# A fused vision-and-text block on one core: the products of the identity that fill TensorE's waits are left out

## What is computed

```python
h = tok(x, W, b, cls_token, pos_embedding)             # patches @ W.T + b, class token, positions
h = concatenate([h, txt], axis=1)                      # 32 x 69 x 256
h = h + attn0(layernorm(h))                            # rotary softmax attention, 16 heads of 16
h = h + ffn0(layernorm(h))                             # 8 experts of 128, top 2 by sigmoid gate, and a shared one
h = h + attn1(layernorm(h))                            # linear attention, layernorm, feed 256-1024-256, layernorm
h = h + ffn1(layernorm(h))                             # 8 experts of 1024, top 2 by softmax
```

## Time and profile before

| | |
|---|---|
| median of three runs | 1016.52 us (1016.45 to 1018.35) |
| the profiled execution | 1020.34 us, of which its span 1018.1 us |
| granted TensorE clock, mean | 0.971 |
| PE busy | 926.0 us, 91% of the span |
| ACT, DVE, POOL busy | 58%, 57%, 62% |

### The profile page before, as it was taken

One profiled execution on the slowest core, in us unless ns is written; L12 is line 12 of the kernel. 1 busy time (PEld: TensorE's weight loads), 2 busy tenths in 40 slices (PEclk: granted clock), 3 DMA queues, 4 the chain that ended last, 5 costly groups with the idle time before them and its releaser, 6 DMA issues. The chain is left out here.

```text
span 1018.1 us, 21166 instructions
## 1 busy us (share of the span) xinstructions
PE 926.0 (91%) x6820; PEld 845.2 (83%) x6820; DVE 576.7 (57%) x1326; ACT 588.6 (58%) x1243; POOL 632.5 (62%) x632
## 2 busy tenths in 40 slices
PE   6997999997999999789879999978999999999980
PEld 5884777776899988579869999867999999999980
DVE  1548999976766663498633666555333333333334
ACT  0432777775666664487445666523766666666644
POOL 3575888875555544253259987611777777778760
PEclk9999999998999999899999999979999999999995
DMA  8773444431311120000080000083566666666657
GB/s 320 250 249 84 148 160 154 159 115 38 110 64 55 47 80 9 1 1 2 1 337 2 17 16 17 16 342 122 158 201 190 198 187 203 206 195 194 192 177 272
DMA packets 66775, 134.60 MB, mean 132 GB/s; under 512 B 12809, under 2 KB 29364, under 8 KB 65524
## 3 DMA queue, kind: packets, MB, share of 16 engines
q1 hardware_dynamic: 58126, 116.49, 35.3%
q0 software_dynamic: 4032, 11.02, 3.0%
q10 hardware_dynamic: 4550, 6.24, 1.8%
HBM read 111.56 MB, written 23.21 MB: 132 GB/s over the span
## 5 line engine op out<-in xcount | busy, mean ns | idle before, releaser
L122 DVE CAST place<-place 128x512 fp32r<-128x512 f32 (+1 forms) x168 | 88.3, 567 | 155.7 <-PE moe_down L128 80.3
L2529 POOL TENSOR_TENSOR place<-place,place 128x512 fp32r<-128x512 f32 x84 | 138.0, 1643 | 50.4 <-DVE place L122 44.7
L2555 PE MATMUL moe_up<-place,place 128*128 128x128 f32 x1344 | 157.0, 275 | 0.5 <-ACT place L2654 0.5
L2555 PEld LDWEIGHTS moe_up<-place,place 128*128 128x128 f32 x1344 | 153.4, 192 | 0.8 <-ACT place L2654 0.8
L128 PE MATMUL moe_down<-place,place 128*128 128x256 f32 x1008 | 132.6, 288 | 4.6 <-DMA place<-w_remainder 2.7
L128 PEld LDWEIGHTS moe_down<-place,place 128*128 128x128 f32 x1008 | 124.8, 193 | 5.1 <-issue 5.1
L2671 ACT ACTIVATE place<-moe_up,place 128x128 f32<-128x128 f32 x336 | 95.1, 367 | 19.0 <-POOL place L2529 14.7
L2658 ACT ACTIVATE place<-place 128x2048 f32 x42 | 80.3, 1913 | 22.4 <-issue 13.1
L1500 POOL TENSOR_TENSOR place<-place,place 128x384 fp32r<-128x384 f32 x42 | 43.9, 1048 | 64.9 <-ACT place L1372 45.0
L1052 PE MATMUL ff_down<-place,place 128*128 128x256 f32 x486 | 69.6, 289 | 4.6 <-POOL place L1500 3.9
L1052 PEld LDWEIGHTS ff_down<-place,place 128*128 128x128 f32 x486 | 61.7, 189 | 11.5 <-POOL place L1500 9.6
(11 more groups left out here) (320 smaller groups left out, 2040.8 us busy)
## 6 DMA issues: line engine op xcount, KB each, us to landing
place<-w_remainder SPq DMA_DIRECT2D x168, 256.0 KB
place<-in_w_dram SPq DMA_DIRECT2D x4, 4096.0 KB, 13.4
place<-gate_rows SPq DMA_DIRECT2D x24, 384.0 KB, 4.9
place<-in_w_dram SPq DMA_DIRECT2D x16, 512.0 KB, 3.7
w_remainder<-place SPq DMA_DIRECT2D x16, 512.0 KB, 2.9
place<-choices SPq DMA_DIRECT2D x5, 768.0 KB, 7.5
place<-value_rows SPq DMA_DIRECT2D x56, 64.0 KB, 2.3
place<-in_patches_dram SPq DMA_DIRECT2D x8, 384.0 KB, 5.6
```

The lines of the kernel that those rows point to most:

```text
L122: return eng.tensor_copy(out, x)
L2529: pool.tensor_tensor(lo[f], raw[f], hi[f].bitcast(F32), ALU.subtract).then_inc(h_split, 1)
L2555: last = pe.matmul(p1[u][k // HK][:, (k % HK) * P:(k % HK + 1) * P], ws[u][:, c, k * P:(k + 1) * P], xT[u][:, c, :], start=(c == 0), stop= ...
```

## The change

All calls of `keep_busy` go, and with them the function. That makes 96 products: 4 at A, 3 at B, 5 at C, 10 at D, 6 at E, 12 at F, 24 at G, 22 at H and 10 at I. Waits, DMAs and the other engines' code stay as they are.

```diff
-def keep_busy(pe, bank, ident, rows, count, fresh=True):
-    for _ in range(count):
-        pe.matmul(bank[:, 0:D], ident, rows, start=fresh, stop=fresh, skip_group_check=True)
...
                         proj(n + 2 - NB)
                         if n == NB - 1:
                             pe.wait_ge(summed, 1)
-                        busy(up[:, 0 if n == NB - 2 else 2, :], 2)
...
                 flip_x(0)
                 pe.wait_ge(summed, 2)
-                busy(up[:, 0, :], 3)
                 logits(0)
                 for n in range(R):
                     rise(n)
                 fall(0)
                 turn_gates(0)
-                busy(turn[:, 1, :], 2)
                 flip_x(1)
-                keep_busy(pe, po[:, 1, D:2 * D], self.ident, self.wo0[:, 0, :], 3, False)
                 logits(1)
...
-                keep_busy(pe, up[:, 0, :], self.ident, self.wo0[:, 0, :], 10)
                 flip_out(NG - 1)
...
                 pe.wait_ge(preset, 7)
-                keep_busy(pe, pc, self.ident, self.wo1[:, 0, :], 6)
                 for a in range(NT + 8):
...
                 proj(0)
                 proj(1)
-                busy(po[:, 0, :], 10)
                 flip_x(0)
-                busy(po[:, 0, :], 2)
                 for n in range(R):
                     rise(n)
...
                 for g in (NG - 2, NG - 1):
-                    busy(up[:, 0, :], 6 if g == NG - 2 else 16)
                     flip_out(g)
-                    busy(up[:, 0, :], 1)
                     logits(g)
...
                 for k in range(2):
-                    keep_busy(pe, idle, self.ident, self.h[:, 0, :], 20 if k == 0 else 2)
                     pe.wait_ge(hot_ready, k + 1)
...
-                keep_busy(pe, p2, self.ident, self.h[:, 0, :], 10)
                 turn_x(0, 0, 0)
                 rise(0, 0)
```

More of the change, by code:

```diff
@@ L1063, in bias_down @@
                         pe.matmul(thirds(po, j), gt_parts[0:3 * ROWS, j * P:(j + 1) * P], e2_b_parts[0:3 * ROWS, :], start=False, stop=False, skip_group_check=True)
-                def busy(bank, count):
-                    keep_busy(pe, bank, self.ident, self.wo0[:, 0, :], count)
                 scores(0)
@@ L2009, in fall @@
                     last.then_inc(fall_mm, 1)
-                def busy(bank, count):
-                    keep_busy(pe, bank, self.ident, self.wo1[:, 0, :], count)
                 proj(0)
                 proj(1)
-                busy(po[:, 0, :], 10)
                 flip_x(0)
-                busy(po[:, 0, :], 2)
                 for n in range(R):
```

## The result

The changed kernel takes 1022.52 us (median of six, 1020.9 to 1023.87), against 1017.09 us for the kernel before (median of six, 1016.45 to 1019.33, the three shown above among them). The ratio is 1.0037, 95% interval 1.0021 to 1.0054: 3.8 us slower, 2.1 to 5.5. The direction is as forecast and the forecast difference, +3.5, lies within the interval. The time itself, 1022.52 us, is 2.5 us above the forecast of 1020.0 and only just inside the range that ended at 1022.6.

A forecast was written before the change was run, and what follows sets the result against it. TensorE, busy nine tenths of the 1018.1 us span, was taken to bound the kernel. The terms A to I summed to +3.5 us, which on the median of 1016.52 gave 1020.0 us, range 1016.6 to 1022.6.

The forecast's parts named there:

- A: Last two sequences of attention, two products after each output projection: both pairs lie on the path, -1.7 us.
- B: Three products before logits(0): covered, and a 4.33 us wait for the gates covers even a slow ramp, 0.
- C: Two products after turn_gates(0), three before logits(1): bias products, rise(4) and proj(2) run at half clock, +1.7 us (0 to 2.7).
- D: Ten products before the last flip_out: nothing won, the turn runs at half clock, +0.6 us (0 to 0.9).
- E: Six products ahead of project(0) in linear attention: on the path behind a 5.20 us wait, -3.1 us.
- F: Second feed, ten products before flip_x(0), two behind: slow turn and rises, partly taken up by waits, +1.2 us (0.6 to 2.2).
- G: 24 products at the second feed's end: last two groups' turns and logits slow, all in one chain, +2.9 us (1.3 to 3.4).
- H: 22 products in the routing: both waits are VectorE's, second half of the table may double, +0.3 us (0 to 0.6).
- I: Ten products starting the routed experts: they hold PE up 0.5 us, but rise(0) stands in the ramp, +1.6 us (0.3 to 2.7).
- rival (1): Only long still waits, not thin stretches, bring the clock down: sum +0.2, 1016.7 us, no change; chance 0.25.
- Rival (2): PE's low clock hardly reaches the path: with no price at all the sum is -4.8, 1011.7 us; chance 0.08.
- Rival (3): Ramps at C, F and I take 2.7 us each, A wins only 0.9: +6.1, 1022.6 us; chance 0.17.

The follow-up runs named there:

- the first experiment: Only the products at A and E left out, the other 86 kept, against the kernel before: 1015.33 against 1020.27 us, ratio 0.9955.
- covered products left out: Products at B, C, D, F, G, H and I left out, A and E kept, against the kernel before: 1027.77 against 1020.27 us, ratio 1.0068.
- the combined version: Against the kernel before: A left out, eight products ahead of the wait at E, eight instead of ten at I; 1010.95 against 1018.24 us, ratio 0.9932.
- the thin kernel: At G, 39 products of 8 columns replace the 24 of 256 columns, against the kernel before: 1027.66 against 1018.24 us, ratio 1.0087.

## Why the prediction was right, and where its terms were off

What each place cost, by the shift of the instruction behind it in the changed kernel, beside the single-place runs:

| place | forecast | changed kernel | by itself |
|---|---|---|---|
| A | -1.7 | -1.7 | -1.7 |
| B | 0 | +0.4 | |
| C | +1.7 | +1.9 | +1.4 |
| D | +0.6 | +0.7 | |
| E | -3.1 | -3.2 | -3.9 |
| F | +1.2 | +0.7 | +0.7 |
| G | +2.9 | +2.6 | +2.6 |
| H | +0.3 | +0.4 | |
| I | +1.6 | +2.0 | +2.7 |
| sum | +3.5 | +3.8 | |

The last column has A and E from the one run that leaves both out; B, D and H were not left out by themselves. C is read at 270.29, where its +2.3 and +1.7 at 263.22 have settled. That the column of the changed kernel adds up to the same 3.8 as the timed ratio is partly luck, since the ratio's interval is 3.4 us wide. And that it comes within 0.3 of the forecast sum is partly luck as well: F and G were too dear by 0.8 together, B, C, D, H and I too cheap by 1.2. The mechanism at each place, though, is what was forecast: products on the path cost their length, and the low clock costs where real work stands in the ramp and no wait takes it up.

**A and E** held: idle products directly behind a wait on the path cost their own length, and at half clock twice that. That the products were what cost at these places is shown in both directions, by leaving them out (-4.6) and by doubling them (+4.1 in the trace). The forecast of E also had its mechanism right that the projections slow down when the products go; with the clock kept by products ahead of the wait the place is worth -5.2 us in the trace, 1.3 to 2.0 us more than leaving them out (-3.9 in the first experiment, -3.2 in the changed kernel).

**C, D and H** came out as worked out in the trace of the changed kernel; only C was also timed alone, and cost more (+3.0) than its trace shows, which is open. **B** was taken as covered, and the wait of 4.4 us did cover PE's slow rises; the +0.4 is in VectorE's chain that makes the gates and may have nothing to do with the clock.

**F** was mis-sized at its last step, "a few short waits behind it take a little more: +1.2". Two traces show +0.7. The rises took 1.8 to 2.0 us longer, and the waits for GpSimd at fall(0) and fall(1) took all of it: the waits behind the first were worth 0.8, not 0.3.

**G** held in its sum. Of its four pieces the turn of group 4 kept full clock here and with G alone left out (+0.3 was half a chance; with all covered products left out it ran slow, +0.5), and the logits took 2.73 us at half clock where 2.8 had been worked out from a mixed row.

**I** was too low: the ramp there measured 2.4 us (6.28 against 3.84) and 2.8 us alone, where 2.1 was taken as the middle of 1.5 to 2.7. The ramp stands wholly in rise(0). The other part of the term, 0.5 us by which the ten products held PE up, isn't shown. The prediction took the bias load as what the first turn's copy needs besides; the turn itself waits for the gathered rows. With the products gone it began 4.62, 4.94 and 5.64 us after GpSimd began the gather, in the changed kernel, with I alone left out and with the covered products left out, and 6.59 us after it in the combined version; in the kernel before it was 5.35. So the rows came later or sooner by 2 us with the gather's code unchanged, and that stands in each reading at I.

Two slips of the prediction move nothing: twelve times 0.43 is 5.2, not 5.1, and rival (1) is given as 1016.7 in one place and 1016.6 in the other.

**What else differs between the two traces is not from the change.** The two profiled executions differ already at the embedding, where no product was removed: in these windows, the first of the kernel before and the second of the changed one, PE retires 18 and 9 products of the same kind in the same time.

```profile
12.79:16.19 3.40, 3.40 (x18) 2.99 (x17) 0.42 (x1) 0.29 (x2) 2.29 (x4) 1.00 0.90 334
```

```profile
12.79:16.19 3.40, 3.40 (x9) 2.68 (x9) 0.42 (x1) 0.56 (x2) 2.36 (x4) 1.00 0.84 316
```

The changed kernel's profiled execution left the half rate later and was 1.9 us late from there on. (The column PEclk prints 1.00 for both; it shows no low clock ahead of the first change that the trace records, and the count of products shows the rate.) In linear attention it won 1.6 us, since the half clock of before at 498.43 was absent, and in the routed experts another 1.0. A further 0.9 was won just ahead of G, by a chance of order between VectorE and GpSimd, in rows of the kernel before and then of the changed one:

```profile
654.57 1.02 POOL L2223 TENSOR_TENSOR place<-place,place 128x384 fp32r<-128x384 f32 x1 [1.39 <-ACT place L2158]
654.59 1.82 DVE L2103 TENSOR_TENSOR place<-place,place 128x768 f32<-128x768 f32 x1
```

```profile
653.88 1.84 POOL L2202 TENSOR_TENSOR place<-place,place 128x384 fp32r<-128x384 f32 x1 [1.39 <-ACT place L2137]
653.88 0.96 DVE L2082 TENSOR_TENSOR place<-place,place 128x768 f32<-128x768 f32 x1
```

The two instructions start within 0.02 us of each other. In each trace one of them takes about 1 us (0.96 or 1.02) and the other 1.82 or 1.84. The long one is VectorE's in the kernel before, and the next normalisation follows from it; in the changed kernel it is GpSimd's. The profiled executions of the kernel with I alone left out and of the combined version gained the same 0.9 us there. All this adds up to -1.2 us with smaller steps, which takes the +3.8 of the places to the 2.6 us between the spans; it is no merit of the forecast.

**The rivals.** Rival (1), that thin stretches leave the clock up, had 0.25 and is refuted: by the thin products at G (0.50 for 17.40 us with PE busy for 16.82), and C alone speaks against it as well: once its five products were gone the clock, fallen ahead of the turn of gates, didn't return until 259.64, and from that turn (248.44) on no wait of PE was longer than 1.60 us. The Trainium skill's rule ("TensorE: Matmul & The Clock Gate", section "Why this matters for your kernels"), that idle gaps beyond some 3 us between bursts halve the clock, fits the long waits at D and F: in the changed kernel it fell at 408.73 within a wait of 5.62 us and at 521.37 within one of 5.82. The wait of 6.96 us at I says nothing of it, since the clock had been low there since 661.31. By that rule the thin kernel, with no wait at G over 1.94 us, would have kept its clock there, and the trace doesn't agree. Rival (2), a clock without a price, is refuted by the covered products alone: +6.9 where it gave -0.5. Rival (3), dearer ramps, was true at I (2.4 to 2.8 us) and false at F (1.8 to 2.0, all taken up by waits) and at A (-1.7).

## What to carry to other kernels

Idle products keep the clock without a price only where they stand ahead of the wait and end before it; behind a wait that sets the path they cost their own length, twice that when the clock is already low. Cost each place by two questions, what real work stands in the ramp behind it and which wait behind that takes the loss up, rather than by the number of products. Products of 8 columns filled the time here but did not hold the clock, and in the one trace at hand filling a wait closer went with a longer wait behind it, so the last place of a chain has to be checked as well.

## What the hardware showed that was not expected

The clock stayed at half while PE issued mostly 8-column products (16.82 of 17.40 us busy). The fall and the return of the clock land at different places from one execution to the next of nearly the same code: at the end of the embedding, where no kernel was changed, the shift lay between -0.1 and +2.3 us, and of the kernels with the same ten products at I some had rise(0) at 3.84 us and others at 5.47. The gathered rows of the routed experts came 4.6 to 6.6 us after the gather began. A single trace therefore prices a place only if the same instruction is followed across it, and even then a late load or a tie between VectorE and GpSimd within the place is counted in. A turn of six transposes took 0.85 to 0.87 us at full and 1.48 to 1.54 at half clock, twelve records of logits 1.50 and 2.73: with short products the cost doesn't quite double.
